# Attention and routed FFN on one core: a batch's routing is spread over the four steps that follow, and the sum of the logits stands one round later

## The chip, the cores and the metric

The kernel runs on 1 core of one Trainium2 chip. The metric is the device time of one execution in microseconds (us); less is better. The median of 3 runs of the kernel before is 1727.35 us.

## What is computed

The reference, cut to what matters (layernorm, a cross attention with 16 heads of 32, and a mixture of 8 experts of which each token takes the best 2):

```python
x = x + xattn(_layernorm(x), ctx, ctx, Wq, bq, Wk, bk, Wv, bv, Wo, bo)      # 8 batches, 512 tokens, D = 512
x = x + ffn(_layernorm(x), router_weight, router_bias, gate_up_proj, ...)   # 8 experts, inner size 512
...
scores = jnp.einsum('bhqd,bhkd->bhqk', Q, K) / np.sqrt(Hd)                  # xattn
attn = jax.nn.softmax(scores, axis=-1)
out = jnp.einsum('bhqk,bhkd->bhqd', attn, V)
...
logits = flat @ router_weight.T + router_bias                               # ffn, the router
scores = jax.nn.softmax(logits, axis=-1)
topk_vals, topk_idx = jax.lax.top_k(scores, K)                              # K = 2
...
glu = gate * jax.nn.sigmoid(gate * ALPHA)                                   # ffn, each expert
act = (up + 1.0) * glu
down = jnp.einsum('tei,eih->teh', act, down_proj) + down_bias
out = jnp.einsum('teh,te->th', down, w)
```

## The kernel before

There are three stages one after the other: attention with the router (some 980 us), a short stage that turns the routing into a list of tiles, and the experts. The change is in the first.

**Units and steps.** The attention's work is cut into 32 units: 8 batches b times 4 quarters c (128 columns, 4 heads). One function, `step(s)`, writes down for each step s (from -2 to 34) what is done in its 8 rounds, numbered 0 to 7. All engines walk through the same list, ORDER, and each does those entries that are its own; an engine does them strictly in this order, and waits on semaphores where an entry needs another engine's result. In step s the kernel computes the exponentials of unit s (`exp`, 2 heads a round), the row maxima of unit s+1 (`max`, one a round), the projections k, q and v of unit s+2, the normalisation (`norm`) of unit s-1, the out projection (`out`) of tokens s-4, their residual and second layernorm (`x2`, `ln2`) and, six steps behind, the router's logits. A step with c = s mod 4 = 1 also turns the next batch's x (`ln1`, `turn_x`), one with c = 2 splits the context (`ctx_hi`, `ctx_lo`). Steps with c = 0 or 3 have neither; they are called **plain steps** below.

**The maxima go through a DMA.** At the start of a step `turn_max` transposes the maxima of unit s on TensorE, ScalarE and VectorE split the result into two parts (m_hi, m_lo), and two DMAs on SP's queue (line 1038) put them into two rows of qs. `exp_scores` of round 1 waits for them (semaphore m_sent).

**The work banks.** Four PSUM banks, work0 to work3, serve every entry but the maxima and the products with v. `Ring` gives them out while ORDER is written down: an entry takes the bank that has been free for longest in ORDER, and holds it until the entry that reads it. `take` on TensorE then waits until the bank's user before has been read. k and q are projected in halves, and hold their bank from the first half until `low` (VectorE's k_lo, q_lo), a round or two later.

**The routing.** For each token tile `logits` makes four partial products (line 464), `logit_sum` adds them with a product of 8 columns (line 470, TensorE) into a work bank, and `logit_out` adds the router's bias (line 761, VectorE) and frees the bank. For each group g of four token tiles (a batch) there follow: `best` 0 and `best` 1 (the first and second expert, lines 830 to 841, six and five small VectorE instructions on 128x32), `count` (lines 847 to 854, six or seven), `soft` (an exponential on ScalarE), `rank` (two products on TensorE into a work bank, lines 477 and 478), `place` (lines 879 to 888, six on VectorE, which frees the bank), `share` (lines 864 to 869 and a DMA), and `list` (two indirect DMAs on GpSimd's queue for each token tile, line 43). GpSimd also sums the exponentials (`add`, lines 962 and 965, 128x1024) and adds the bias to the residual (`bo`, line 954).

Of the kernel before, what the change touches and what calls it, by code (L numbers as in the profile page):

```python
# [31 lines left out]
def route_groups(n_tiles, batch):  # L32

    last = n_tiles - 2 * batch
    return [(n, batch) for n in range(0, last, batch)] + [(last, batch - 1), (last + batch - 1, batch + 1)]
# [33 lines left out]
def attention_stage(nc, x, ctx_t, w_t, bq, bk, bv, bo, router_wt, router_b, out, xln_dram, w_rows, w_stored, token_list, listed, stored, route, ident):  # L69
    B, S, D = x.shape  # L70
    C = D // P
    T = S // P
# [9 lines left out]
    GROUPS = route_groups(B * T, T)  # L82
    groups = range(len(GROUPS))
# [3 lines left out]
    with ExitStack() as ctx:  # L87
# [62 lines left out]
        best = sb("best", [P, TOP_K, SLOTS])  # L150
# [21 lines left out]
        def step(s):  # L172
# [3 lines left out]
            def at(r, *keys):  # L176
                rounds[r] += keys
# [22 lines left out]


            if s - 6 in tokens[:-T]:
                at(0, ("logit_sum", s - 6))
                at(1, ("logit_out", s - 6))
            if s - 5 in tokens[:-T]:
                at(0, ("x2", s - 5))
                at(1, ("rstd", s - 5))
# [12 lines left out]
                at(2, ("bo", s))  # L220


            for r, lag, *keys in ((1, 9, ("best", 0)), (2, 9, ("best", 1)), (3, 9, ("count",)), (5, 9, ("soft",)),
                                  (2, 10, ("rank",)), (3, 10, ("place",)), (1, 11, ("share",))):
                g, odd = divmod(s - lag, T)
                if g in groups[:-2] and not odd:
                    at(r, *[(kind, g, *what) for kind, *what in keys])
            g, t = divmod(s - 11, T)
            if g in groups[:-3]:
                at(3, ("list", g, t))  # L230
            if s == units[-1]:
                at(2, ("list", groups[-3], 0))
                at(3, ("list", groups[-3], 1))
# [17 lines left out]
            g = groups[-2]  # L251
# [74 lines left out]

        tokens = range(B * T)
        ORDER = [key for s in range(-2, B * C + 3) for key in step(s)]


# [66 lines left out]
        at = {key: n for n, key in enumerate(ORDER)}  # L397
# [539 lines left out]
        def on_pool(e):  # L937
# [39 lines left out]
            for n, (width, step, first, by_partition) in enumerate(places):  # L977
                begin = sum(place[0] for place in places[:n])
                e.iota(consts_i[:, begin:begin + width], [[step, width]], base=first, channel_multiplier=by_partition).then_inc(s_route, 1)
# [903 lines left out]
```

## Time and profile before

| what | value |
|---|---|
| time, median of 3 runs | 1727.35 us |
| the runs | 1725.28, 1727.35, 1731.16 us |
| span of the profiled execution | 1724.2 us |
| what lies around the span, against the median | 3.15 us |
| TensorE (PE) busy | 1599.4 us, 93% |
| VectorE (DVE) busy | 1274.8 us, 74% |
| ScalarE (ACT) busy | 658.4 us, 38% |
| GpSimd (POOL) busy | 837.4 us, 49% |
| granted TensorE clock, mean | 0.969 |

The profile is of one execution. Its own total is not given beside its span, so the span stands for it, and the median is compared with it. PE is TensorE, PEld its weight loads, DVE VectorE, ACT ScalarE, POOL GpSimd, SP the engine whose queue issues most DMAs. A row of the timeline gives start, duration, engine, line, what is written from what, how many instructions are merged in it, and in brackets the idle time just before it and what ended it. Line numbers are those of the kernel before; in the kernel after all lines behind the change stand 4 higher.

### The profile page before, as it was taken

The numbers are of one execution on the slowest core, as the hardware profiler recorded it, in microseconds if no ns is written. First come the engines' busy times: TensorE is split into PE (matmuls) and PEld (weight loads), VectorE is DVE, ScalarE is ACT, GpSimd is POOL, SyncE is SP. The second block draws the span as 40 slices with busy tenths as digits, with TensorE's granted clock in tenths as the row PEclk, the third lists the DMA queues.
The fourth block names the chain that finished last, engine by engine and source line by source line (L and its number), as shares of the span: only waits on it lengthen the run. The fifth ranks groups of instructions, "written<-read, shape, count | busy, mean of one in ns | idle before, by whom it ended". The sixth has DMA issues, their size and how long they took to land. (4 is left out here: it accounts for less than half of the span.)

```text
span 1724.2 us, 30241 instructions
## 1 busy us (share of the span) xinstructions
PE 1599.4 (93%) x9612; PEld 1167.5 (68%) x9612; DVE 1274.8 (74%) x2410; ACT 658.4 (38%) x1271; POOL 837.4 (49%) x638
## 2 busy tenths in 40 slices
PE   5898999999999999999998469999999999999995
PEld 3555555555555555555553269999999998999994
DVE  3675777878768778787685677777878778777873
ACT  3353544545445445444434133223333233223320
POOL 4364656566566676666777322333333333333232
PEclk9999999999999999999999769999999999999997
DMA  6342433343434434433331161324443363324321
GB/s 218 81 119 70 111 102 96 105 106 89 127 80 113 103 96 100 116 85 100 97 89 32 59 221 62 100 87 166 160 153 119 93 214 107 106 85 151 115 86 62
DMA packets 101061, 188.99 MB, mean 110 GB/s; under 512 B 28192, under 2 KB 29600, under 8 KB 100896
## 3 DMA queue, kind: packets, MB, share of 16 engines
q1 hardware_dynamic: 79936, 124.25, 25.1%
q0 software_dynamic: 20960, 62.76, 11.4%
q8 instruction: 77, 1.26, 0.4%
q14 instruction: 88, 0.72, 0.2%
HBM read 204.32 MB, written 37.51 MB: 140 GB/s over the span
## 5 line engine op out<-in xcount | busy, mean ns | idle before, releaser
L782 DVE TENSOR_REDUCE negmax<-max_ps 128x2 f32<-128x1024 f32 x256 | 312.2, 1219 | 163.3 <-PE max_ps L535 163.0
L659 ACT ACTIVATE pt<-work 128x512 f32<-128x512 f32 x512 | 278.3, 594 | 251.1 <-PE work L547 242.5
L965 POOL TENSOR_TENSOR acc<-acc,pt 128x1024 f32<-128x1024 f32 x128 | 303.7, 2377 | 128.4 <-ACT pt L659 128.3
L1467 PE MATMUL gu_ps<-xgT_hi,wg_hi 128*128 128x256 f32 x1248 | 349.3, 280 | 1.5 <-DVE xgT_lo L1582 1.5
L1467 PE MATMUL gu_ps<-xgT_lo,wg_hi 128*128 128x256 f32 x1248 | 345.8, 277 | 0.0
L1467 PE MATMUL gu_ps<-xgT_hi,wg_lo 128*128 128x256 f32 x1248 | 345.6, 277 | 0.0
L962 POOL TENSOR_TENSOR acc<-pt 128x1024 f32<-128x1024 f32 x64 | 153.3, 2397 | 196.8 <-PE work L567 129.3
L1728 POOL DMA_INDIRECT out<-acc,token_of x78 | 77.0, 987 | 331.4 <-DVE acc L1626 325.9
L1467 PEld LDWEIGHTS gu_ps<-xgT_hi,wg_hi 128*128 128x128 f32 x1248 | 235.2, 188 | 2.0 <-issue 1.9
L1467 PEld LDWEIGHTS gu_ps<-xgT_lo,wg_hi 128*128 128x128 f32 x1248 | 235.5, 189 | 0.1
L1467 PEld LDWEIGHTS gu_ps<-xgT_hi,wg_lo 128*128 128x128 f32 x1248 | 235.2, 188 | 0.0
L535 PE MATMUL max_ps<-ks,qs 96*128 96x512 f32 x512 | 199.7, 472 | 25.8 <-DVE negmax L782 13.5
L1537 ACT ACTIVATE sig<-gate 128x256 f32<-128x256 f32 x156 | 65.1, 417 | 325.1 <-DVE gate L1590 325.1
L547 PE MATMUL work<-qs,ks 98*128 98x512 f32 x512 | 169.5, 408 | 11.7 <-DVE q_lo L769 5.7
L535 PEld LDWEIGHTS max_ps<-ks,qs 96*128 96x128 f32 x512 | 88.7, 193 | 88.7 <-issue 53.7
L559 PE MATMUL o_ps<-pt,v 128*32 128x512 f32 x1024 | 138.7, 614 | 1.6 <-ACT pt L659 1.6
L1481 PE MATMUL d_ps<-wd_hi,hid_hi 128*128 128x512 f32 x312 | 125.8, 403 | 12.1 <-DVE acc L1623 11.7
L1723 POOL DMA_INDIRECT acc<-out,token_of x78 | 81.1, 1040 | 103.0 <-DMA out<-acc,token_of 90.6
L547 PEld LDWEIGHTS work<-qs,ks 98*128 98x128 f32 x512 | 97.1, 192 | 47.3 <-issue 12.1
L1481 PE MATMUL d_ps<-wd_lo,hid_hi 128*128 128x512 f32 x312 | 125.3, 402 | 0.0
L502 PE MATMUL work<-xT,wq 128*128 128x512 f32 x256 | 125.0, 611 | 0.0
L1481 PE MATMUL d_ps<-wd_hi,hid_lo 128*128 128x512 f32 x312 | 124.9, 400 | 0.0
(219 smaller groups left out, 2891.9 us busy)
## 6 DMA issues: line engine op xcount, KB each, us to landing
raw_g<-w_gate_up SPq DMA_DIRECT2D x39, 2048.0 KB
raw_d<-w_down SPq DMA_DIRECT2D x39, 1024.0 KB
ks<-k_hi SPq DMA_DIRECT2D x252, 64.0 KB
qs<-q_hi SPq DMA_DIRECT2D x252, 64.0 KB
bd<-b_down SPq DMA_DIRECT2D x39, 256.0 KB
x_in<-x SPq DMA_DIRECT2D x36, 256.0 KB, 3.3
ctxT_raw<-ctx_t SPq DMA_DIRECT2D x32, 256.0 KB, 4.1
xln_dram<-x SPq DMA_DIRECT2D x32, 256.0 KB, 2.7
```

Of the source, the lines that this page charges most:

```text
L502: ins = e.matmul(to[:, :], wq[:, k, cols], xT[:, k, :], start=(k == 0), stop=(k == C - 1))
L535: ins = e.matmul(max_ps[:, j, :], qs[i][0:3 * HD, h, t * P:(t + 1) * P], ks[i][0:3 * HD, h, :], start=True, stop=True)
L547: e.matmul(to[:, :], ks[i][0:3 * HD + 2, h, k * P:(k + 1) * P], qs[i][0:3 * HD + 2, h, :], start=True, stop=True).then_inc(exp_ready.sem, 1)
L559: ins = e.matmul(o_ps[u % 2][HD * h:HD * (h + 1), :], v[:, k, c * P + HD * h:c * P + HD * (h + 1)], pt[k % 2][:, h, :], start=(k == 0), st ...
L659: e.activation(pt[k % 2][:, h, :], in_work("exp", u, k, h)[:, :], ACT.Exp, scale=scale).then_inc(exped.sem, 1)
L782: e.tensor_reduce(negmax[:, u % 2, n:n + 2], max_ps[:, :, :], AX.X, ALU.max, negate=True).then_inc(maxed.sem, 1)
L962: e.tensor_tensor(acc[:, heads, :], pt[0][:, heads, :], pt[1][:, heads, :], ALU.add).then_inc(added.sem, 1)
L965: e.tensor_tensor(acc[:, heads, :], acc[:, heads, :], pt[k % 2][:, heads, :], ALU.add).then_inc(added.sem, 1)
L1467: ins = e.matmul(gu_ps[n % GU_BANKS][:, part, :], wg[s][pw][:, k, cols], xgT[s][px][:, k, :], start=(k == 0 and m == 0), stop=(k == KD - 1 ...
L1481: ins = e.matmul(d_ps[j][:, :], hid[s][px][:, k, j * P:(j + 1) * P], wd[s][pw][:, k, :], start=(k == 0 and m == 0), stop=(k == KF - 1 and ...
L1723: e.indirect_dma_start(out=acc[s][:, j, :], out_offset=None, in_=out_rows, in_offset=slot_rows(i, j)).then_inc(acc_in[s], 16)
L1728: e.indirect_dma_start(out=out_rows, out_offset=slot_rows(i, j), in_=acc[i % 2][:, j, :], in_offset=None).then_inc(scattered.sem, 16)
```

## The change

`logit_sum` stands in round 1 and `logit_out` in round 2 of its step, one round later than before (not in step 32). For the groups 0 to 3 the routing is spread: `best` 0 stands in round 3 of step 4g+9 (c = 1), `best` 1 in round 3 of step 4g+11 (c = 3), `count` in round 3 of step 4g+12 (c = 0), `rank` and `place` in rounds 0 and 1 of step 4g+13 (c = 1), `share` in round 1 of step 4g+15, and the lists in round 3 of the steps 4g+14 to 4g+17. Groups 4 and 5 stay close together; their `best` 0 and 1 stand one round later. No instruction is added or left out.

```diff
             if s - 6 in tokens[:-T]:
-                at(0, ("logit_sum", s - 6))
-                at(1, ("logit_out", s - 6))
+                first = 0 if s == B * C else 1
+                at(first, ("logit_sum", s - 6))
+                at(first + 1, ("logit_out", s - 6))
...
-            for r, lag, *keys in ((1, 9, ("best", 0)), (2, 9, ("best", 1)), (3, 9, ("count",)), (5, 9, ("soft",)),
-                                  (2, 10, ("rank",)), (3, 10, ("place",)), (1, 11, ("share",))):
-                g, odd = divmod(s - lag, T)
-                if g in groups[:-2] and not odd:
-                    at(r, *[(kind, g, *what) for kind, *what in keys])
-            g, t = divmod(s - 11, T)
-            if g in groups[:-3]:
-                at(3, ("list", g, t))
+            spread = (3, 9, "best", 0), (3, 11, "best", 1), (3, 12, "count"), (5, 12, "soft"), (0, 13, "rank"), (1, 13, "place"), (1, 15, "share")
+            dense = (2, 9, "best", 0), (3, 9, "best", 1), (3, 9, "count"), (5, 9, "soft"), (2, 10, "rank"), (3, 10, "place"), (1, 11, "share")
+            for some, timed in ((groups[:-4], spread), (groups[-4:-2], dense)):
+                for r, lag, kind, *what in timed:
+                    g, odd = divmod(s - lag, T)
+                    if g in some and not odd:
+                        at(r, (kind, g, *what))
+            for g in groups[:-3]:
+                t = s - GROUPS[g][0] - (14 if g in groups[:-4] else 11)
+                if 0 <= t < T:
+                    at(3, ("list", g, t))
```

The order of the instructions follows from this list, and so do the banks. Three places are shown.

First, TensorE in rounds 0 and 1 of step 12 (c = 0) in the kernel before. max_ps is the row maxima's bank pair, qs and ks the operands of the scores, wk_hi and ctxT_hi those of the k projection; of its six products in a round the first stands. Before:

```order
L547 MATMUL work3<-qs2,ks2 128x512 [waits parts_made]
L470 MATMUL work0<-select,parts 128x8 [waits parts_made,m_lo_made]
L494 MATMUL work2<-ctxT_hi,wk_hi 128x512 [waits exped]
...
L547 MATMUL work3<-qs0,ks0 128x512 [waits m_sent,exped]
L547 MATMUL work1<-qs0,ks0 128x512 [waits x2_made]
L559 MATMUL o_ps1<-pt1,v 32x512 [waits exped]
```

The same place in the changed kernel:

```order
L551 MATMUL work3<-qs2,ks2 128x512 [waits parts_made]
L498 MATMUL work2<-ctxT_hi,wk_hi 128x512 [waits m_lo_made]
...
L551 MATMUL work0<-qs0,ks0 128x512 [waits m_sent,exped]
L551 MATMUL work3<-qs0,ks0 128x512 [waits exped]
L563 MATMUL o_ps1<-pt1,v 32x512 [waits exped]
L563 MATMUL o_ps1<-pt1,v 32x512 x3
L474 MATMUL work1<-select,parts 128x8 [waits parts_made,x2_made]
```

The sum of the logits (line 470, now 474) has gone from round 0 to the end of round 1's products with v, and the k projection takes the bank of the turned maxima in place of that of an exponential.

Second, TensorE in round 2 of the same step, two score products and the first half of the q projection. Before:

```order
L547 MATMUL work3<-qs0,ks0 128x512 [waits exped]
L547 MATMUL work1<-qs0,ks0 128x512 [waits exped]
L502 MATMUL work0<-xT,wq 128x512 [waits logits_out]
L502 MATMUL work0<-xT,wq 128x512
L535 MATMUL max_ps<-ks1,qs1 128x512 [waits maxed]
```

In the changed kernel:

```order
L551 MATMUL work0<-qs0,ks0 128x512 [waits exped]
L551 MATMUL work3<-qs0,ks0 128x512 [waits exped]
L506 MATMUL work0<-xT,wq 128x512 [waits exped]
L506 MATMUL work0<-xT,wq 128x512
L539 MATMUL max_ps<-ks1,qs1 128x512 [waits maxed]
```

The q projection took the bank that the logits' sum had left; now it takes work0, which the first score product of the same round has just filled.

Third, VectorE in rounds 1 to 3 of step 13 (c = 1). Before:

```order
L761 TENSOR_TENSOR logits<-work1,rb_rows 128x8
L830 TENSOR_REDUCE best<-logits 128x4
L832 TENSOR_TENSOR ranks<-logits,best 128x32
...
L769 SCALAR_TENSOR_TENSOR k_lo<-work0,bk_col,k_hi 128x512
L782 TENSOR_REDUCE negmax<-max_ps 128x2
L746 TENSOR_SCALAR x2<-x2,mv,rstd 128x512
L847 TENSOR_TENSOR hots<-hot0,hot1 128x32
L848 TENSOR_TENSOR expo<-logits,best 128x32
L854 TENSOR_TENSOR before<-before,hots 128x8 x4
```

In the changed kernel:

```order
L883 TENSOR_TENSOR ranks<-work1,consts 128x32
L887 TENSOR_TENSOR hot0<-hot0,ranks 128x32
...
L786 TENSOR_REDUCE negmax<-max_ps 128x2
L765 TENSOR_TENSOR logits<-work3,rb_rows 128x8
L773 SCALAR_TENSOR_TENSOR k_lo<-work0,bk_col,k_hi 128x512
L786 TENSOR_REDUCE negmax<-max_ps 128x2
L750 TENSOR_SCALAR x2<-x2,mv,rstd 128x512
L834 TENSOR_REDUCE best<-logits 128x4
L836 TENSOR_TENSOR ranks<-logits,best 128x32
```

The place of a group stands where its `best` 0 stood, nothing stands where `best` 1 did, and `best` 0 stands in the place of `count`. In TensorE's round 2 of this step the second score product now takes the bank that `place` frees.

## Rows read from the trace of the kernel before

**Rows 1.** The page, busy time: us (share of the span) xinstructions.

```profile
PE 1599.4 (93%) x9612; PEld 1167.5 (68%) x9612; DVE 1274.8 (74%) x2410; ACT 658.4 (38%) x1271; POOL 837.4 (49%) x638
```

**Rows 2.** Windows of steps 5, 12, 13: length, busy PE, PEld, DVE, ACT, POOL, clock, DMA.

```profile
185.30:215.00 29.70, 28.86 (x156) 16.86 (x154) 20.49 (x26) 16.28 (x29) 19.51 (x11) 1.00 0.40 114
384.50:411.50 27.00, 26.67 (x142) 15.58 (x140) 19.27 (x31) 11.80 (x22) 16.62 (x13) 1.00 0.34 89
411.50:442.00 30.50, 29.15 (x157) 17.05 (x156) 25.54 (x44) 16.40 (x30) 21.31 (x13) 1.00 0.42 105
```

**Rows 3.** Timeline of TensorE, step 12, rounds 0 to 3.

```profile
385.50 0.29 PE L470 MATMUL work<-select,parts 128*128 128x8 f32 x2
386.12 0.50 PE L494 MATMUL work<-ctxT_hi,wk_hi 128*128 128x512 f32 x1 [0.33 <-ACT pt L659]
...
388.08 0.63 PE L547 MATMUL work<-qs,ks 98*128 98x512 f32 x2
...
392.07 1.88 PE L502 MATMUL work<-xT,wq 128*128 128x512 f32 x4
393.39 1.02 PE L535 MATMUL max_ps<-ks,qs 96*128 96x512 f32 x2
```

**Rows 4.** Timeline of ScalarE, step 12, rounds 0 to 2.

```profile
385.46 1.09 ACT L659 ACTIVATE pt<-work 128x512 f32<-128x512 f32 x2 [0.43 <-PE work L547]
...
391.34 0.69 ACT L643 ACTIVATE k_hi<-work,bk_col 128x512 fp32r<-128x512 f32 x1 [1.75 <-PE work L494]
392.04 1.08 ACT L659 ACTIVATE pt<-work 128x512 f32<-128x512 f32 x2
```

**Rows 5.** Timeline of TensorE, step 5, round 1 (no logits yet).

```profile
189.02 0.70 PE L547 MATMUL work<-qs,ks 98*128 98x512 f32 x2 [0.64 <-DMA qs<-m_lo]
```

**Rows 6.** Timeline of SP, step 12, and line 1038's time to landing.

```profile
385.94 0.58 SPq L1038 DMA_DIRECT2D qs<-m_lo  x1
```

```profile
DMA to landing us min/median/max: 1.8/1.8/2.5
```

**Rows 7.** Timeline of all engines, step 13, rounds 1 to 3.

```profile
417.71 1.28 POOL L954 TENSOR_TENSOR x<-x,bo_rows 128x512 f32<-128x512 f32 x1
...
418.45 0.59 DVE L832 TENSOR_TENSOR ranks<-logits,best 128x32 f32<-128x32 f32 x1
...
419.21 1.88 PE L502 MATMUL work<-xT,wq 128*128 128x512 f32 x4
...
420.31 1.07 ACT L659 ACTIVATE pt<-work 128x512 f32<-128x512 f32 x2
...
421.14 0.73 PE L535 MATMUL max_ps<-ks,qs 96*128 96x512 f32 x2
...
424.46 2.37 DVE L848 TENSOR_TENSOR expo<-logits,best 128x32 f32<-128x32 f32 x1
```

**Rows 8.** Timeline of VectorE, step 14, round 3: the place of group 1.

```profile
453.61 0.18 DVE L879 TENSOR_TENSOR ranks<-work,consts 128x32 f32<-128x32 f32 x1
...
454.72 0.17 DVE L888 CAST pos<-pos_f 128x8 int32<-128x8 f32 x1
```

**Rows 9.** Timeline of VectorE and GpSimd, step 12, round 3.

```profile
395.59 0.54 DVE L746 TENSOR_SCALAR x<-x,mv,rstd 128x512 f32<-128x512 f32 x1
399.15 1.23 DVE L782 TENSOR_REDUCE negmax<-max_ps 128x2 f32<-128x1024 f32 x1 [3.02 <-PE max_ps L535]
```

```profile
396.93 2.36 POOL L962 TENSOR_TENSOR acc<-pt 128x1024 f32<-128x1024 f32 x1 [3.38 <-PE work L567]
```

**Rows 10.** Timeline of TensorE: step 9, round 3, and step 14, round 3.

```profile
307.73 0.72 PE L535 MATMUL max_ps<-ks,qs 96*128 96x512 f32 x2 [0.77 <-DVE negmax L782]
```

```profile
451.41 0.73 PE L535 MATMUL max_ps<-ks,qs 96*128 96x512 f32 x2 [0.79 <-DVE negmax L782]
```

**Rows 11.** Step 25: TensorE's wait in round 5, and the window behind it.

```profile
774.36 0.50 PE L547 MATMUL work<-qs,ks 98*128 98x512 f32 x1 [1.31 <-DVE q_lo L769]
```

```profile
774.00:779.00 5.00, 4.64 (x23) 2.98 (x24) 2.92 (x5) 1.31 (x3) 2.36 (x1) 0.66 0.44 105
```

## Prediction

> **What bounds the kernel now.** I read the page first: TensorE is busy for 93% of the span, VectorE for 74% [rows 1]. Then the windows of single steps. A plain step (12) is 27.0 us long and TensorE is busy for 26.67 of them at full clock [rows 2]; so a plain step is TensorE's own queue, and any wait put into that queue lengthens it. A step with c = 1 (13) takes 30.5 us, of which TensorE is busy for 29.15; step 5 has the same c and no routing yet, and takes 29.7 [rows 2]. So all the routing costs about 0.8 us in one step of four, less than the change's size suggests.
>
> Last I read TensorE's row order inside a step. In round 0 the k projection waits 0.33 us for an exponential, after the logits' sum of 0.29 us [rows 3]. In round 1 the first score product starts at 388.08 [rows 3]. It needs the maxima: m_lo is issued at 385.94 and lands 1.8 us later at best, at about 387.75 [rows 6]. So that product has about 0.3 us of room ahead of it, no more; and in step 5, where no logits' sum stands in round 0 and k takes the turned maxima's bank as it will now, the score product waits for just this DMA, 0.64 us [rows 5].
>
> **The change part by part.**
>
> *Round 0, the logits' sum leaves.* TensorE reaches the k projection 0.62 us earlier (0.29 of the sum, 0.33 of the wait, rows 385.50 and 386.12) [rows 3]. The gain is 0 to 0.3 us a step, what the DMA leaves; step 5 shows the wait moving to the score product of round 1 [rows 5]. I take 0: the maxima's chain starts with the step's first instruction and is not touched.
>
> *Round 1, the sum comes back.* It stands behind the products with v, where TensorE has no gap. Its price is its own 0.29 us [rows 3]. From below it can be 0.2 (part of its weight loads lie under other products), from above 0.4 (the two rows do not show what it would cost without the wait behind it).
>
> *Round 2, the q projection's bank.* Before, the bank was free since round 1. Now it is the one that the first score product of the same round has filled, so q waits until ScalarE has read it. ScalarE does k_hi first, at 391.34, and starts the two exponentials at 392.04 [rows 4]. One of the two takes 0.59 us by its mean (1.08 for the overlapping pair), so it ends at 392.63. In round 0 the same pattern shows the handover: pair at 385.46, its first ends at 386.05, the projection starts at 386.12 [rows 3, 4]. So q starts at 392.70 in place of 392.07 [rows 3]: 0.63 us, with bounds of 0.5 and 0.75. Behind it everything on TensorE is shifted, since the rest of the step has no gap [rows 2]. This holds for twelve plain steps, 7 to 28: 12 x (0.29 + 0.63) = 11.0 us.
>
> *Steps with c = 2* (6, 10, 14, 18, 22, 26). They project q in round 0 and k in round 3, so no bank trap; the sum costs 0.29. TensorE waits in round 3 for VectorE, whose reduction itself follows TensorE's round 2 [rows 10], so the shift goes through. 6 x 0.29 = 1.7 us. In step 26 the rank of group 4 now takes a bank that waits for an exponential of its round behind q_hi and ctx_hi: about 0.7 us more.
>
> *Steps with c = 1 and a place* (13, 17, 21). Here `place` stands in round 1 of VectorE and frees the bank of round 2's second score product; q takes that of the first. ScalarE has two 128x512 copies ahead (ln1), and starts the pair at 420.31 [rows 7]; with the sum ahead 0.29 later, its first ends at 421.2. q then starts at 421.25 in place of 419.21, and the next maxima's product, 1.32 us behind it as in the plain step (392.07 to 393.39) [rows 3], at about 422.5 in place of 421.14 [rows 7]: 1.4 us. `place` takes 1.3 us (453.61 to 454.89) where GpSimd is idle [rows 8]. Beside GpSimd's bias addition it takes about 0.6 more, as `ranks` of line 832 took 0.59 and ended with it [rows 7]: it ends near 420.0, before q's bank, so it hides behind ScalarE's. In round 3 `best` 0 replaces `count`. The count's long instruction, 2.37 us [rows 7], lasts as long as GpSimd's sum beside it; `best` 0 meets the same sum with its fifth instruction, and comes out 0.2 us better against the shifted TensorE. I take 1.3 us: 3 x 1.3 = 3.9 us; bounds 0.9 and 1.7 each.
>
> The Trainium skill, page "SBUF — State Buffer", section "Who interferes with whom", says that a VectorE operation with two inputs in SBUF and a GpSimd operation that reads SBUF exclude each other for the whole instruction, and that a reduction never does. The two rows of 0.59 and 2.37 us agree. By the rule alone the place's two products in the new round would be held to the end of the bias addition and `place` would end near 420.0; with no such lock near 419.5. The sum is the same by both, because ScalarE is later; the rule speaks against this new place all the same.
>
> *The other c = 1 steps.* Step 9 has no place; its maxima's product of round 3 stands at 307.73 after a wait of 0.77 for VectorE [rows 10], a wait that goes, so only 0.6 is left. Step 25 has place in round 1 and `best` 0, `best` 1 and `count` behind in rounds 2 and 3, one round more crowded than before: 2.4 us. Step 29 has `best` 1 and `count` together in round 3, some 4.2 us on VectorE (one instruction of 2.37, ten of about 0.19) against the 3.0 that a plain step leaves it [rows 7 to 9]: 1.1 us. Sum 4.1; bounds 1.8 and 7.
>
> *The routing in round 3 of plain steps* (11, 12, 15, 16, ...). VectorE is free from 396.13 to 399.15, and GpSimd's sum starts at 396.93 [rows 9]. `count` fits: 1.3 us, its two-input float instruction ahead of the sum. `best` 1's last instruction comes under the sum, ends near 399.5, and makes q_lo 0.35 late: 0.3 us in four steps, 1.2 us; bounds 0 and 4. SP and GpSimd's queues: the lists are the same two DMAs a step; in steps 27 to 29 four, and they fall into the 3.38 us that GpSimd is idle [rows 9]. `share` moves whole steps into the same kind of round. Nothing for these. What the spread takes away (`best` in rounds 1 and 2 of c = 1, `place` in round 3 of c = 2) is in the numbers above; the latter was hidden.
>
> **Sum:** 11.0 + 1.7 + 0.7 + 3.9 + 4.1 + 1.2 = 22.6 us. Span 1724.2 + 22.6 = 1746.8. The median of the runs stands 3.15 above this span, so 1750 us, 1.3% slower. The stages behind start later by as much and are not touched.
>
> **The rivals.**
> *Faster (0.12).* The mechanism is the first round's wait. If the score product of round 1 follows TensorE rather than the maxima's landing, round 0 gives 0.62 and round 1 takes 0.29: 0.33 in 18 steps, 6 us, and c = 1 steps fall toward step 5's length, 0.8 in five, 4 us: 1717 us. It needs a landing 0.3 us earlier than 387.75, and a q that waits under 0.33 us in round 2; from there on it decides. Step 5's row speaks against it.
> *No change (0.06).* q's wait is caught by a gap that the modelled ends of products hide, and round 0's gain pays for the sum: 1727 us, up to 1731. For it: a busy TensorE is not one at its peak. Against: the rounds 3 to 7 of all plain steps have the same length.
> *Only the sum (0.07).* The q wait is hidden but the 0.29 us stand in 25 steps: 7 us, 1734.
> *The clock falls as well (0.15).* Step 25 shows it: a wait of 1.31 us, then 5 us with a granted clock of 0.66, some at 1.2 and some at 2.4 GHz, which costs 0.34 x 5 = 1.7 us [rows 11]. The changed c = 1 steps have some 2 us of waits in round 2. If the clock falls in each of the four with a place, 7 us more, and in some plain steps too: 1757 to 1765. Against: waits of 0.6 and 0.3 us did not lower it.
> The Trainium skill, page "TensorE: Matmul & The Clock Gate", Part 1, says that the clock drops to half when the array has been idle and comes back with work. The row of step 25 agrees; by the rule alone the change would add such falls, and the sum would be this rival's.
>
> **How the numbers follow.** The forecast itself has 0.60. Its own range is 1741 to 1760: the low bounds add up to 8.4 + 1.2 + 0.3 + 2.7 + 1.8 + 0 = 14.4, the high ones to 13.8 + 2.4 + 1.0 + 5.1 + 7 + 4 = 33.3. With the clock and the sum alone the range is 1735 to 1764; it leaves out the first two rivals, 0.18. A measurement of this kernel tells about 0.3% (5 us) from no change. Slower by more: 0.60 + 0.15 + 0.07 = 0.82; within: 0.06; faster: 0.12.
>
> **What would show it.** Right: plain steps of 27.9 us; in them q's product with an idle time of about 0.6 ended by ScalarE's pt; the first score product of round 1 with an idle time ended by the DMA qs<-m_lo; line 474 between the products with v and k; c = 1 steps with a place near 31.8. Wrong: plain steps still at 27.0, or q's product starting 0.46 us behind the score products.

## The result, and the profile after

The changed kernel took 1746.76 us (median of 6 runs, 1742.48 to 1754.41). The kernel before took 1729.87 us beside it (6 runs, 1725.28 to 1737.38). The ratio is 1.0102, with a 95% interval of 1.0078 to 1.0125: slower by 1%. Two single executions of later kernels, of 3126.67 and 8777.85 us, lie far outside all others and are left out of the medians below. The profiled execution has a span of 1745.4 us against 1724.2, which is 21.2 more; the sum had said 22.6.

The page of the changed kernel, busy time, and two of its groups (busy and mean ns | idle time before them and what ended it):

```profile
PE 1601.0 (92%) x9612; PEld 1160.8 (67%) x9612; DVE 1275.8 (73%) x2410; ACT 660.4 (38%) x1271; POOL 838.5 (48%) x638
...
L551 PE MATMUL work<-qs,ks 98*128 98x512 f32 x512 | 173.0, 413 | 23.0 <-DMA qs<-m_lo 12.0
...
L506 PE MATMUL work<-xT,wq 128*128 128x512 f32 x256 | 126.7, 618 | 9.6 <-ACT pt L663 8.3
```

The same two groups in the kernel before:

```profile
L547 PE MATMUL work<-qs,ks 98*128 98x512 f32 x512 | 169.5, 408 | 11.7 <-DVE q_lo L769 5.7
...
L502 PE MATMUL work<-xT,wq 128*128 128x512 f32 x256 | 125.0, 611 | 0.0
```

Against [rows 1], no engine has more work: TensorE went from 1599.4 to 1601.0 us. So all but some 2 of the 21 us are waiting. The two groups say where: the q projection (line 506) waited for nothing before, and now waits 8.3 us for exponentials; the score products (551) wait 12.0 us for the DMA of the maxima, and by the source view of line 547 it was 5.3 us before. Against this the k projection waits less.

Windows of steps 5, 12, 13 and 30 of the changed kernel, columns as in [rows 2]:

```profile
184.40:214.00 29.60, 28.74 (x156) 16.77 (x154) 20.49 (x26) 16.31 (x29) 19.52 (x11) 1.00 0.39 109
387.00:414.80 27.80, 26.93 (x140) 15.30 (x139) 19.94 (x37) 11.94 (x23) 14.52 (x11) 1.00 0.33 86
414.80:446.60 31.80, 29.38 (x159) 17.17 (x158) 25.03 (x39) 16.42 (x29) 19.30 (x11) 1.00 0.37 108
...
913.30:941.00 27.70, 24.04 (x101) 10.80 (x99) 18.19 (x30) 11.55 (x23) 18.61 (x12) 0.82 0.09 29
```

Step 5 has no logits and kept its 29.6 us. The plain step went from 27.0 to 27.8, step 13 from 30.5 to 31.8 [rows 2]. In step 30 the granted clock is 0.82; we come back to that.

Timeline of TensorE, step 12, rounds 0 to 2, of the changed kernel (start, duration, what; in brackets the idle time before it and what ended it):

```profile
387.54 0.63 PE L551 MATMUL work<-qs,ks 98*128 98x512 f32 x2
388.01 0.40 PE L498 MATMUL work<-ctxT_hi,wk_hi 128*128 128x512 f32 x1
...
390.43 0.70 PE L551 MATMUL work<-qs,ks 98*128 98x512 f32 x2 [0.41 <-DMA qs<-m_lo]
...
392.06 0.39 PE L474 MATMUL work<-select,parts 128*128 128x8 f32 x2
...
394.25 0.63 PE L551 MATMUL work<-qs,ks 98*128 98x512 f32 x2
395.33 1.98 PE L506 MATMUL work<-xT,wq 128*128 128x512 f32 x4 [0.46 <-ACT pt L663]
```

Timeline of ScalarE, same stretch:

```profile
393.98 0.69 ACT L647 ACTIVATE k_hi<-work,bk_col 128x512 fp32r<-128x512 f32 x1 [1.96 <-PE work L498]
394.68 1.09 ACT L663 ACTIVATE pt<-work 128x512 f32<-128x512 f32 x2
```

and of VectorE, the logit_out in its new round:

```profile
395.59 0.15 DVE L765 TENSOR_TENSOR logits<-work,rb_rows 128x8 f32<-128x8 f32 x1
```

Read it beside [rows 3, 4]. The k projection starts 0.47 us behind the score product, with no wait. The 0.62 us gained there end at 390.43, where the score product waits for the maxima. The logits' sum (474) stands behind the products with v. Then q starts 1.08 us behind the score products instead of following them; k_hi is ahead of the exponentials on ScalarE.

The following table is worked out from the starts of TensorE's products for the next step's maxima (line 535 before, 539 after): the length of a round, or of rounds 3 to 7 and the whole step, in the changed kernel minus that before, us. The first row has medians.

| | round 0 | round 1 | round 2 | rounds 3 to 7 | step |
|---|---|---|---|---|---|
| plain steps 8, 12, 16, 24, 28 | -0.72 | +0.84 | +0.73 | 0 | +0.85 |
| step 13 (c = 1, with place) | -0.01 | +0.15 | +1.29 | -0.20 | +1.22 |
| step 9 (c = 1, no place) | -0.71 | +0.79 | +0.57 | +0.29 | +0.94 |

Steps 6 to 29 sum to +16.6 us: +7.6 in the twelve plain steps, +3.2 in those with c = 2, +5.9 in those with c = 1. The start is 1.0 us earlier in this execution, and 5.6 us come behind step 29.

### The profile page after: what moved, and what is told of

Same layout as the page of the kernel before. It is cut to its first block and busy times, and to the rows that moved or that the text cites. A ratio compares the mean times of both kernels' runs of the same rounds, so it can differ in the third digit from the quotient of the medians.

```text
span 1745.4 us, 30247 instructions
## 1 busy us (share of the span) xinstructions
PE 1601.0 (92%) x9612; PEld 1160.8 (67%) x9612; DVE 1275.8 (73%) x2410; ACT 660.4 (38%) x1271; POOL 838.5 (48%) x638
## 5 line engine op out<-in xcount | busy, mean ns | idle before, releaser
L551 PE MATMUL work<-qs,ks 98*128 98x512 f32 x512 | 173.0, 413 | 23.0 <-DMA qs<-m_lo 12.0
```

Of the source, the lines that this page charges most:

```text
L551: e.matmul(to[:, :], ks[i][0:3 * HD + 2, h, k * P:(k + 1) * P], qs[i][0:3 * HD + 2, h, :], start=True, stop=True).then_inc(exp_ready.sem, 1)
```

## The experiments

Each kernel was timed beside the kernel before on the same chip. Three edits are told apart: A, logit_out one round later, which keeps a bank busy, so that q takes a bank of its own round; B, the logits' sum one round later in TensorE's order; C, the routing spread over a batch. Step lengths below are worked out as in the table above.

**Only the logits late.** The kernel before with A and B (`best` 0 had to follow to round 2, beside `best` 1):

```
-                at(0, ("logit_sum", s - 6))
-                at(1, ("logit_out", s - 6))
+                first = 0 if s == B * C else 1
+                at(first, ("logit_sum", s - 6))
+                at(first + 1, ("logit_out", s - 6))
```

> Only the logits are moved: logit_sum in round 1, logit_out in round 2 (best 0 and best 1 one round later, since they read it); the rest of the routing stands as before. Theory A, the bank: the q projection of round 2 waits for the exponential of its own round. It expects plain steps of 27.8 us as in the changed kernel (12 times 0.85 = 10 us), 0.3 to 0.8 us in c = 2 steps (the rank now takes such a bank too, 4 us), and c = 1 steps that are longer than in the changed kernel, since best and count crowd rounds 2 and 3 (like its step 25; 1.5 to 2.5 us each, 9 us): 1.012 to 1.015 of before. Theory C, the spread's places on VectorE cost the time: 1.000 to 1.003.

Measured: 1750.43 us against 1726.67, ratio 1.0133 (1.0104 to 1.0162); plain step 27.83. The plain steps have their whole 0.85 us without any spread. The c = 1 steps 9 to 29 lengthen by 0.2 to 2.5, where 1.5 to 2.5 was expected. Steps 10, 18, 22 and 26 lengthen by 1.9 to 2.3, where 0.3 to 0.8 was; 0.6 of that stands in round 2, where rank takes a bank of its own round too. In the changed kernel only step 26 has a rank there. In step 18 the rest stands in round 7. In steps 10, 22 and 26 another 1.3 us stands in round 3, and that is the clock. Step 26 of this kernel, TensorE and a window:

```profile
815.69 0.19 PE L478 MATMUL work<-hots,tri 128*128 128x32 bf16 x1 [1.37 <-ACT pt L660]
...
816.87 1.94 PE L560 MATMUL o_ps<-pt,v 128*32 128x512 f32 x8
```

```profile
816.00:821.00 5.00, 5.00 (x23) 1.50 (x23) 3.28 (x9) 1.70 (x4) 0.38 (x1) 0.66 0.35 79
```

and the same place in the changed kernel:

```profile
810.15 0.19 PE L481 MATMUL work<-hots,tri 128*128 128x32 bf16 x1 [1.37 <-ACT pt L663]
...
811.31 1.06 PE L563 MATMUL o_ps<-pt,v 128*32 128x512 f32 x8
```

The wait is the same 1.37 us in both, but here the granted clock fell behind it and there it did not. The profile with only the logits late has five such falls in steps 10 to 26 (rounds 3 of 10, 22 and 26, round 2 of 13 and of 25). The mean clock was 0.967 or 0.968 in all four executions, and 0.972 at the median in the kernel before beside them; in the changed kernel's six it was 0.967 to 0.974, with a median of 0.971. The two kernels' total ratios, 1.0133 and 1.0102, have intervals that overlap, so that the spread saves something of what the late out costs is likely, and not shown.

**Only the spread.** The changed kernel with the logits in rounds 0 and 1, as before (C alone).

```
-                first = 0 if s == B * C else 1
-                at(first, ("logit_sum", s - 6))
-                at(first + 1, ("logit_out", s - 6))
+                at(0, ("logit_sum", s - 6))
+                at(1, ("logit_out", s - 6))
```

> Only the routing is spread; logit_sum and logit_out stand in rounds 0 and 1 as before. Theory A expects plain steps of 26.97 us as before, c = 2 steps as before, and c = 1 steps with a place 0.3 to 1 us longer (k waits for the second exponential of round 0, q for the place; the count is gone from round 3 and gives 0.45 back): 0.999 to 1.003 of before. Theory C expects most of the loss here: 1.007 to 1.011.

Measured: 1731.16 us, ratio 1.0018 (1.0001 to 1.0035); plain step 26.97, as before. Step 9 is 1.1 us shorter; steps 13, 17 and 21 are 0.3 to 0.8 longer. The profiled execution took 1736.58 us, 5 more than the median, so its step lengths say less than the median does. The spread costs little or nothing, and brings nothing.

**The out back in round 1.** The changed kernel without A (B and C stay):

```
-                at(first + 1, ("logit_out", s - 6))
+                at(1, ("logit_out", s - 6))
```

> The changed kernel with logit_out back in round 1, behind a logit_sum that stays in round 1, so that its bank is free again for q. Theory A expects the q product 0.46 us behind the score products without a wait, plain steps of 27.1 us (0.15 for the sum's own time), c = 2 steps 0.25 longer than before, and c = 1 steps some 0.8 us longer than before (q takes the place's bank): 1.003 to 1.005 of before, that is a good half of the change's loss gone. Theory B, the sum's instructions in round 1 are what costs, expects the changed kernel's 1.010.

Measured: 1727.73 us, ratio 1.0015 (0.9998 to 1.0031); plain step 27.11. Timeline of TensorE, step 12, of this kernel:

```profile
385.15 0.70 PE L551 MATMUL work<-qs,ks 98*128 98x512 f32 x2 [0.42 <-DMA qs<-m_lo]
...
386.77 0.39 PE L474 MATMUL work<-select,parts 128*128 128x8 f32 x2
...
388.97 0.63 PE L551 MATMUL work<-qs,ks 98*128 98x512 f32 x2
389.44 1.88 PE L506 MATMUL work<-xT,wq 128*128 128x512 f32 x4
```

The sum stands at its new place and the score product waits the same 0.42 us, but q follows the score products at once. One entry of the order, a VectorE addition of 0.15 us, carries most of the loss. The 0.13 us that a plain step keeps are B. The ratio came out below the expected 1.003 to 1.005, and steps 13, 17 and 21 are 0.0, 0.2 and 0.6 us longer than before, where 0.8 was expected.

**Only the bank held.** The kernel before with A alone: TensorE's order is untouched, only the bank is released a round later, so that `Ring` gives q another one (`best` 0 in round 2):

```
                 at(0, ("logit_sum", s - 6))
-                at(1, ("logit_out", s - 6))
+                at(1 if s == B * C else 2, ("logit_out", s - 6))
```

> The kernel before with logit_sum still in round 0 and only logit_out in round 2 (best 0 and 1 one round later): TensorE's instructions stand exactly as before, only the bank is held longer. Theory A expects q's wait of 0.7 us in round 2 of the plain steps (27.7 us), the rank's wait in c = 2 and longer c = 1 steps as in the run with the logits late: 1.010 to 1.014 of before. Theory B expects 1.000, since nothing moves on TensorE.

Measured: 1746.81 us, ratio 1.0106 (1.0080 to 1.0132); plain step 27.69, the +0.71 us all in round 2. TensorE in step 12 of this kernel:

```profile
398.15 0.63 PE L547 MATMUL work<-qs,ks 98*128 98x512 f32 x2
399.23 1.12 PE L502 MATMUL work<-xT,wq 128*128 128x512 f32 x2 [0.45 <-ACT pt L659]
```

The same gap of 1.08 us as in the changed kernel (the last row shows two of q's four products). A alone makes a slowdown of the same size; it is not what TensorE does in another order, but when a bank becomes free. The parts are not quite the same: in a plain step A makes 0.71 of the 0.85 us, and steps 10, 14 and 26 are 1.8 to 1.9 us longer here. Of that, 0.6 is the rank's wait in round 2, and in steps 10 and 26 another 1.3 stands in round 3, as in the kernel with only the logits late.

**The place, with the out early.** As the third kernel, and rank and place of groups 0 to 2 moved from rounds 0 and 1 of c = 1 to rounds 2 and 3 of c = 2:

```
+            early = spread[:4] + ((2, 14, "rank"), (3, 14, "place")) + spread[6:]
-            for some, timed in ((groups[:-4], spread), (groups[-4:-2], dense)):
+            for some, timed in ((groups[:-5], early), (groups[-5:-4], spread), (groups[-4:-2], dense)):
...
-                t = s - GROUPS[g][0] - (14 if g in groups[:-4] else 11)
+                t = s - GROUPS[g][0] - (15 if g in groups[:-5] else 14 if g in groups[:-4] else 11)
```

> The changed kernel with logit_out back in round 1 (as in e3), and with rank and place of the spread groups 0 to 2 moved from rounds 0 and 1 of a step with c = 1 to rounds 2 and 3 of a step with c = 2. In e3 the steps 13, 17 and 21 kept an idle time of 0.5 to 0.8 us in round 2, which I put down to the place beside GpSimd's bias addition. If that is right, steps 13 and 17 come out 0.6 to 1.1 us shorter than before's (all routing gone from them but nothing added), plain steps stay at 27.1, and the total is 1722 to 1727 us, ratio 0.998 to 1.000. If the idle time of round 2 is instead the exponential's alone (the two bias copies ahead of it on ScalarE), steps 13 and 17 stay within 0.2 us of e3's, and the ratio stays at 1.001 to 1.002.

Measured: 1725.36 us against 1730.17, ratio 0.9982 (0.9961 to 1.0002); steps 13 and 17 take 29.59 and 29.58 us, 1.0 and 1.1 less than before. Their round 2 has no idle time left. So in the third kernel the place in round 1 was what q waited for (0.51 us in its step 13, ended by `pos`, line 892).

**The place, with the out late.** The same move of rank and place, in the changed kernel (the edit is the last one's).

> The changed kernel (logit_out late, in round 2) with rank and place of groups 0 to 2 moved back to rounds 2 and 3 of a step with c = 2. The prediction said that in steps 13, 17 and 21 the place in round 1 hides behind ScalarE, since q waits for its own round's exponential behind the two ln1 copies. If so, round 2 of steps 13 and 17 keeps its idle time of 1.2 to 1.5 us and the steps stay within 0.3 us of the changed kernel's 31.8; steps 14, 18 and 22 get about 0.6 longer, since rank now takes a bank of its own round as in step 26; total 1747 to 1750, ratio 1.010 to 1.013. If the place is the later of the two, the idle time of round 2 falls to 0.5 to 0.9, the steps to 30.9 to 31.2, and the total stays at the changed kernel's 1745 to 1747.

Measured: 1741.18 us against 1726.13, ratio 1.0092 (1.0068 to 1.0117). Step 13 takes 31.69 us against the changed kernel's 31.78, and q still waits there. TensorE of this kernel, step 13:

```profile
420.99 0.63 PE L552 MATMUL work<-qs,ks 98*128 98x512 f32 x2
423.33 1.12 PE L507 MATMUL work<-xT,wq 128*128 128x512 f32 x2 [1.72 <-ACT pt L664]
```

and of the changed kernel, where the wait is in two pieces, 0.75 for the place and 0.71 for the exponential:

```profile
423.31 0.50 PE L551 MATMUL work<-qs,ks 98*128 98x512 f32 x1 [0.75 <-DVE pos L892]
424.52 1.98 PE L506 MATMUL work<-xT,wq 128*128 128x512 f32 x4 [0.71 <-ACT pt L663]
```

(The row at 423.33 shows two of q's four products.) With the place gone the wait is one piece of 1.72 us, in place of 1.46 us in two, and the step is as long within 0.1. So with the bank held late the place hides behind ScalarE, as the prediction had it; its cost shows only once the bank comes early. The total came out lower than expected here (1741 where 1747 to 1750 stood, ratio 1.0092 where 1.010 to 1.013 did; the kernel before took 1726.13 us beside this one and 1729.87 beside the changed kernel, and the intervals of the two ratios overlap). In the profiled execution rank does cost its 0.6 us in round 2 of steps 14, 18 and 22 against the changed kernel, of which round 3 gives 0.3 back, but round 7 of step 14 is 2.4 us shorter. The other executions were not profiled.

**The sum in the gap, in the kernel before.** Only the place of the sum in round 1 is new, between the product for the maxima and the score product:

```
                     at(r, ("max", s + 1, r))
+                if r == 1 and s != B * C and s - 6 in tokens[:-T]:
+                    at(r, ("logit_sum", s - 6))
...
-                at(0, ("logit_sum", s - 6))
+                if s == B * C:
+                    at(0, ("logit_sum", s - 6))
                 at(1, ("logit_out", s - 6))
```

> The kernel before with the routing where it was, and only the sum of the logits moved from round 0 to the place between round 1's product for the maxima and its first score product (logit_out stays in round 1). If the gap holds it: plain steps 26.8 us, 18 to 22 steps x 0.14 = 3 us less in all, ratio 0.997 to 0.999. If not (the sum pushes the score products back by 0.29, round 0 gives back nothing beyond that): 26.97 to 27.1 and ratio 1.000 to 1.003.

Measured: 1726.52 us (11 runs) against 1730.17, ratio 0.9982 (0.9964 to 1.0001); plain step 26.90, 0.06 to 0.10 less than before, where 0.14 was expected. The gap takes the sum.

**Everything that helped.** The last edit and the place's move, logit_out in round 1:

> As e5, and the sum of the logits stands in round 1 between the product for the maxima and the first score product, where TensorE waits 0.41 us for the DMA of the maxima in the changed kernel; logit_out in round 1, so that q's bank is free in time. If that wait is the DMA's alone, the sum of 0.29 us fits into it: plain steps of 26.8 us, 0.14 less than before's, and 1718 to 1723 us in all, ratio 0.996 to 0.998. If the score product follows TensorE's own queue, the plain step stays at 27.1 and the ratio at e5's.

Measured: 1719.41 us (8 runs, 1716.89 to 1723.22) against 1730.17, ratio 0.9947 (0.9924 to 0.9971): faster than before by half a per cent. The profiled span is 1718.6. Windows of steps 12 and 13, and TensorE in round 1 of step 12:

```profile
382.80:409.60 26.80, 26.54 (x140) 15.53 (x139) 19.94 (x37) 11.91 (x23) 14.50 (x11) 1.00 0.33 89
409.60:439.40 29.80, 28.94 (x158) 17.20 (x156) 23.52 (x33) 16.28 (x29) 19.31 (x11) 1.00 0.40 115
```

```profile
385.18 0.63 PE L542 MATMUL max_ps<-ks,qs 96*128 96x512 f32 x2
385.65 0.29 PE L477 MATMUL work<-select,parts 128*128 128x8 f32 x2
386.20 0.70 PE L554 MATMUL work<-qs,ks 98*128 98x512 f32 x2 [0.26 <-DMA qs<-m_lo]
...
389.78 0.63 PE L554 MATMUL work<-qs,ks 98*128 98x512 f32 x2
390.24 1.88 PE L509 MATMUL work<-xT,wq 128*128 128x512 f32 x4
```

The score product comes 3.43 us behind the step's first product (382.77), within 0.01 of the changed kernel's 3.44 (386.99 to 390.43): the DMA decides, and the sum is carried under its wait. In this version the spread does bring something. Steps 13 and 17 are 0.8 and 1.0 us shorter than before, where the kernel with the sum in the gap alone has 0.0.

## Why the prediction was right

The sign and the mechanism came out as forecast. The total did too, but in part by luck: the steps that the sum covers were 6 us less than it said, and 5.6 us came behind them that it had at nothing. By its steps:

- **Round 0.** The gain was taken at 0, between bounds of 0 and 0.3. The wait came (0.41 us). But the score product stands 3.44 us behind the step's first product (390.43 and 386.99), and before it stood 3.60 behind (388.08 and 384.48 in its timeline): a gain of 0.16, the middle of the bounds. With the sum's 0.29 that leaves the +0.12 of rounds 0 and 1, where +0.29 stood: 2 us too much over twelve steps.
- **Round 2, q's bank.** 0.63 forecast, 0.73 measured, inside the bounds. That A alone makes it is shown by the kernel with only the bank held (+0.71) and by the one without A (0). The delay itself was read rightly: q starts 1.08 us behind the score products, 0.46 before, so 0.62 later. The other 0.10 is in q's four products, which take 1.98 us behind the wait and took 1.88 without it [rows 3]. The idle time itself is 0.46 and not the 0.6 that was named as the sign: the score products' merged row lasts 0.63 of the 1.08 us.
- **Twelve plain steps.** 0.85 in place of 0.92 each; with the steps behind a c = 2 step, where the start is noisy (-0.30 in step 11, +0.21 in 15), 7.6 us in place of 11.0. That is under the forecast's own low bound of 8.4, which had left out the gain of round 0.
- **Steps with c = 2.** 3.2 us for 2.4. The rank in step 26 cost 0.59 of its 0.7 in round 2, for the reason given, and round 3 gave 0.32 of it back. The rest is scatter of round 7 and one late landing of the maxima in step 22 (0.94 us of waiting). From issue to landing this DMA took 1.8 us at the median and 3.3 at the longest.
- **Steps 13, 17 and 21.** 1.3 each forecast, 1.22, 1.07 and 1.54 measured. Round 2 cost 1.3 to 1.5 and round 3 another 0.3; round 5 gave 0.42 to 0.45 back, which I had not seen. A likely reason is that with `count` gone from round 3 VectorE reaches q's low part earlier.
- **The place beside GpSimd.** Right in mechanism: it hides behind ScalarE, shown by the pair of kernels with the place moved. GpSimd's additions did stand beside it, and stretched its products (below).
- **Steps 9, 25 and 29.** 0.94, 0.49 and 0.63 measured for 0.6, 2.4 and 1.1. In step 25 the fall of the clock that the kernel before showed [rows 11] did not occur in the changed kernel's profile. That alone gave 1.6 us back, though its wait is still there (1.34 us); without it the step would have been 2.1 longer, near the forecast. The wait and the window behind it, in the changed kernel:

```profile
788.83 0.50 PE L551 MATMUL work<-qs,ks 98*128 98x512 f32 x1 [1.34 <-DVE q_lo L773]
```

```profile
789.00:794.00 5.00, 5.00 (x35) 3.40 (x36) 3.15 (x5) 2.44 (x6) 2.38 (x1) 1.00 0.48 102
```

- **Routing in round 3 of plain steps.** 1.2 forecast, 0 measured. From round 3 on, steps 11 to 24 with `best` 1 or `count` in round 3 are as long as steps 7, 8 and 28 without, within 0.02 in each of rounds 3 to 6, both in the changed kernel and in the kernel with only the spread. This term was wrong: `best` 1 does stretch beside GpSimd's sum (2.39 us in step 15), but it delays nothing on TensorE.

So the sum to step 29 was too high by 6 us, the start was 1.0 us shorter, and 5.6 us came behind step 29 that the prediction left at nothing: this is the term that was furthest off. Of the 5.6, 2.4 are in step 30, where the clock went to half. It fell in that step before the change too, for a shorter time; the window there, in the kernel before:

```profile
897.70:925.00 27.30, 21.42 (x104) 9.98 (x103) 20.53 (x35) 11.74 (x23) 20.36 (x13) 0.94 0.11 35
```

TensorE in that step of the changed kernel, at 1.2 GHz by the length of its products, and two of the same lines a little later:

```profile
921.84 1.22 PE L539 MATMUL max_ps<-ks,qs 96*128 96x512 f32 x2 [0.38 <-DVE negmax L786]
...
923.85 1.94 PE L563 MATMUL o_ps<-pt,v 128*32 128x512 f32 x8
...
929.76 0.73 PE L539 MATMUL max_ps<-ks,qs 96*128 96x512 f32 x2 [0.85 <-DVE negmax L786]
...
930.90 1.07 PE L563 MATMUL o_ps<-pt,v 128*32 128x512 f32 x8
```

The rival with the clock was right that falls cost microseconds, but they came in step 30 (and one in round 0 of step 15, which the kernel before has too) and not in the steps with a place: there waits of 1.5 us in two pieces left the clock at 1.00. So did the single wait of 1.72 us in the kernel with the late out and the place moved; the window of its step 13:

```profile
414.70:446.40 31.70, 29.05 (x156) 16.86 (x155) 23.14 (x33) 16.89 (x31) 18.31 (x10) 1.00 0.38 109
```

The length of a wait alone does not decide, then; the two profiles of step 26 above say the same. That the change itself made the falls of step 30 or took that of step 25 away is not shown. The third kernel and the one with the place moved have the same TensorE and VectorE entries in both steps. Yet round 3 of step 30 takes 5.58 us in the first of them and 2.99 in the second (changed kernel 5.58, before 2.99), and round 5 of step 25 takes 5.95 and 7.48 (changed kernel 5.95, before 7.56). And the mean clocks of the changed kernel and of the one before are alike (above). The rest of the 5.6 us, 1.8 in the last steps and 1.4 in the expert stage, was not taken apart. The total agrees with the sum within 1.4 us because these errors have opposite signs. The forecast median, 1750, lies 3.2 above the measured one: 1.4 from the sum, and 1.8 because the median stands 1.4 us above the profiled span here, where 3.15 was added.

**The rivals.** The first one, faster, named its condition: a landing 0.3 us earlier and a q that waits under 0.33 us. The gain was 0.16 and q starts 0.62 later. The kernel without A shows the other side: with q's wait gone and the sum at its new place, the time is that of before within 0.2%, so round 0's gain alone would not have made the kernel faster. "No change" fails with the interval of the ratio, 1.0078 to 1.0125. "Only the sum" fails with the kernel in which the sum did not move and the time was the changed kernel's.

## What to carry to other kernels

Moving an instruction by one slot moves the life of its buffer as well: list, for each rotating bank, who fills it next and who must have emptied it, and look for a user that now waits for something started in its own slot. On an engine with 0.3 us of idle time in 27, one addition of 0.15 us that releases a bank one round later cost 1%. And a wait that the trace shows to be a DMA's is a place where small work of the same engine can stand for almost nothing: against the kernel before, the same sum cost 0.13 us a step behind that gap and gave 0.1 us when it stood in it.

## What the runs showed of the hardware

A wait costs TensorE a little more than its own length. Behind a wait the first 128x512 product shows 0.50 us, and 0.40 where none stands ahead of it (386.12 in [rows 3] and 388.01 above); the pair of score products shows 0.70 for 0.63. The starts agree: the next product for the maxima comes 1.42 us behind q's first where q waited and 1.32 where it did not. That is the 0.10 missing from the q term. A wait is not the only cause: with none ahead, but behind the products with v, the k projection's first product in step 12 of the kernel before shows 0.51 as well (389.63).

VectorE's small operations beside GpSimd, in the changed kernel. First the timeline of step 13 (place), then GpSimd's, then two lines' durations over the kernel (ns, minimum, median, maximum):

```profile
421.60 1.01 DVE L887 TENSOR_TENSOR hot<-hot,ranks 128x32 f32<-128x32 f32 x2
...
429.49 2.40 DVE L842 TENSOR_TENSOR hot<-expert_less,pick 128x32 f32<-128x32 f32 x1
```

```profile
421.06 1.28 POOL L958 TENSOR_TENSOR x<-x,bo_rows 128x512 f32<-128x512 f32 x1
429.47 2.36 POOL L966 TENSOR_TENSOR acc<-pt 128x1024 f32<-128x1024 f32 x1 [7.14 <-PE work L571]
```

```profile
L852 DVE TENSOR_TENSOR expo<-logits,best x8: 178/186/195, 399.5 to 999.4; 128x32 f32<-128x32 f32 x6, 128x24 f32<-128x24 f32 x1, 128x40 f32<-128x40 f32 x1
```

```profile
L858 DVE TENSOR_TENSOR before<-before,hots x32: 161/163/2294, 399.6 to 1000.3; 128x8 bf16<-128x8 bf16 x32
```

An operation of 0.19 us ends with GpSimd's addition when the two meet: 2.40 us beside the sum of 2.36. The first of the place's two products took 0.8 us and not 0.19, and ended with the bias addition (the row at 421.60 holds both). The same product of line 852 that took 2.37 us before [rows 7] takes 0.19 everywhere now, since it stands ahead of the sum; another took its place in the queue. By the Trainium skill, page "SBUF — State Buffer", section "Who interferes with whom", a VectorE operation with two inputs in SBUF and a GpSimd one that reads SBUF exclude each other. The rows agree. What I had not expected is how small the stretched operation can be: 128x8 in bf16, 0.16 us, became 2.29.
